# Attention steps relaid over the engines, and the softmax reciprocals turned in the value product's bank

## Chip, cores and metric

The kernel runs on one core of a Trainium2 chip. The metric is the device time of one execution in microseconds (us), as the median of several runs.

## What is computed

The reference is one transformer block on x of shape (2, 512, 256), with a modulation from c:

```
mod = (silu(c) @ wmod) -> sa, ca, ga, sb, cb, gb
h = layernorm(x) * (1 + ca) + sa
x = x + ga * attn(h)          # 32 query heads, 8 kv heads, width 64, rope, sinks, window of 128
h = layernorm(x) * (1 + cb) + sb
h2 = h + attention(rmsnorm(h))  # 32/8 heads again, causal over 512, no window
x = x + gb * (h2 + moe(rmsnorm(h2)))   # 8 experts, top 2
```

Everything is float32; the kernel splits each matmul operand into a high part and a low part (rounded value and rest) and adds three products: high by high, low by high, high by low.

## The kernel before

**Stages.** A prologue loads and prepares; then one software pipeline of 128 attention steps runs; then routing, the experts (lines 1075 and 1096) and the output. Steps 0 to 63 are the first attention (two batches of 32 steps, called windowed), steps 64 to 127 the second (causal). The four functions `step_window` and the four `step_causal` (tensor, scalar, vector; gpsimd and sync have one `step`) write out by hand what each engine does in step u. Every engine works its own list in order; semaphores join them.

**One step u** handles a tile of 128 queries t = u % 4 of a group of four heads. `scores(u, j)` (line 882) for j = 0 to 3 fills one of two banks psS; `mask_max(u, j)` on VectorE (line 1481) adds the mask and takes the maximum; `exp_head` on ScalarE (line 1167) makes the probabilities in pbuf. Score j waits until the mask of score j - 2 has freed the bank. Two steps later `turn_probs(u, k)` (line 892) transposes key tile k into a bank psX, ScalarE copies its high part (`probs_hi`, pTh), VectorE subtracts to get the low part (`probs_lo`, line 1497, pTl), and `values(u, k)` (line 917) multiplies with v and adds up in psO. A windowed tile has one or two key tiles, a causal one up to four.

**The division.** `denominator(u)` on VectorE makes rden, the four reciprocals of a row (in the windowed steps with a term of the sink: `sink_in` on GpSimd, line 682, an exp on ScalarE, and den, line 1489). GpSimd spreads rden over 256 columns (`spread`, line 694, rdenx), TensorE turns that (`turn_scale`, line 900), ScalarE copies it to rS (`scale_of`), and VectorE multiplies psO by rS (`scale_out`, line 1503, oS). ScalarE copies the high part oh (`out_hi`), GpSimd subtracts (`out_low`, line 687), and `out_project` (line 933) adds the product with wo in psY.

**Projections.** `ahead(u)` names the piece of a coming group's q, k or v that step u computes: 14 of 16 steps have one (a run of 16 steps is a quad; m = u % 16). `project_q`, `project_k` and `project_v` (lines 817, 830, 847) write the bank psP. The turned scale of `turn_scale` and the turned features of `turn_features` (line 859) are written into psP too, so a projection first waits until ScalarE has copied rS out of it (`begin_item`):

```
                if u is not None and u >= 2:
                    pe.wait_ge(a_rx, min(u - 1, NU))
```

The windowed half sends a q or k piece through `rope` on VectorE (lines 1448 and 1450), then GpSimd adds, copies the high part and subtracts (lines 661 to 675) into st. In the causal half ScalarE and VectorE split it straight from psP into st. SyncE stores st to DRAM (qd, kd) and loads it back in another layout (qE, kT), one buffer of st being used by all. The weights are loaded raw and split on GpSimd (`split_wq`, `split_wkv`, `split_wo`: a copy, then a subtraction).

## Time and profile before

| | us |
|---|---|
| median of 3 runs | 1406.89 (1406.08 to 1414.29) |
| the profiled execution, whole | 1400.63 |
| its span, first to last instruction | 1398.7 |

In the page of the profile, PE is TensorE's matmuls and PEld its weight loads, DVE VectorE, ACT ScalarE, POOL GpSimd. Over the span PE was busy 1064.0 us (76%), DVE 792.3 (57%), ACT 712.4 (51%) and POOL 478.8 (34%), and the mean granted TensorE clock was 0.905 of full speed. A matmul's end is modelled, so busy PE says that matmuls were in flight. "Idle before" is how long the engine stood still just ahead of a group of instructions; "issue" is what the profile gives where it finds no releaser.

### The profile page before, as it was taken

Reading aid. Unit: us, or ns where it says so; the run is one execution under the profiler, and the core shown is the slowest. Engines: PE = TensorE matmul, PEld = TensorE weight load, DVE = VectorE, ACT = ScalarE, POOL = GpSimd, SP = SyncE. Lnnn points to the kernel's source line nnn. Section 1 sums busy time; section 2 is a strip of 40 time slices with the busy share of each in tenths; the row PEclk is TensorE's granted clock in tenths of the full one; section 3 lists DMA queues with packets and bytes.
Section 4 is the critical chain, followed back from the end, with each engine's and each line's share of the span. In section 5 each row is a group of like instructions: output and inputs, shape, how many; then the busy total and the mean of one; then the engine's idle time right before and its main releaser. Section 6 shows DMA issues by size and latency. Waiting matters only on the chain.

```text
span 1398.7 us, 22967 instructions
## 1 busy us (share of the span) xinstructions
PE 1064.0 (76%) x6836; PEld 946.2 (68%) x6836; DVE 792.3 (57%) x2276; ACT 712.4 (51%) x2003; POOL 478.8 (34%) x659
## 2 busy tenths in 40 slices
PE   3647767777775677779878999988899726889893
PEld 1336666667665566668767888877788616888883
DVE  4445565555555554456655666656666553666655
ACT  2124535455453454566665666675676523555541
POOL 2355544755653454244222424322222140000003
PEclk7778978999997798999999999999999957999997
DMA  6455445545731343454344345534332063555513
GB/s 144 124 121 166 129 128 140 164 131 163 168 93 46 98 123 96 132 135 142 89 123 99 99 121 135 145 84 128 84 88 49 1 227 105 155 144 151 151 39 104
DMA packets 151823, 166.58 MB, mean 119 GB/s; under 512 B 79572, under 2 KB 108180, under 8 KB 146580
## 3 DMA queue, kind: packets, MB, share of 16 engines
q1 hardware_dynamic: 129427, 143.27, 38.8%
q10 hardware_dynamic: 20736, 17.64, 3.9%
q0 software_dynamic: 1536, 4.20, 0.9%
q8 instruction: 57, 0.93, 0.3%
q14 instruction: 67, 0.54, 0.1%
HBM read 106.28 MB, written 58.79 MB: 118 GB/s over the span
## 4 chain that ended last, share of the span: by engine, by line
PE 37%; issue 8%; DVE 6%; ACT 4%; DMA 3%; POOL 2%; ACTq 1%; SPq 0%; DVEq 0%; POOLq 0%
PE psO L917 7%; PE psS L882 5%; PE psX L892 4%; PE psP L817 4%; PE psS L1075 3%; PE psX L1075 3%; PE psY L933 3%; DMA kd<-st 2%; PE psO L1096 2%; PE psP L1096 2%; ACT pTh L1136 1%; DVE pbuf L1481 1%; PE psP L900 1%; DVE pTl L1497 1%; POOL xg L766 1%
## 5 line engine op out<-in xcount | busy, mean ns | idle before, releaser
L1167 ACT ACTIVATE pbuf<-pbuf,nmax 128x256 f32<-128x256 f32 (+3 forms) x512 | 265.5, 519 | 298.0 <-DVE nmax L1481 296.7
L1481 DVE CUSTOM_DVE_ANT_0 pbuf<-psS,mcau 128x256 f32<-128x256 f32 (+3 forms) x512 | 215.4, 437 | 55.8 <-PE psS L882 52.4
L1497 DVE TENSOR_TENSOR pTl<-psX,pTh 128x512 fp32r<-128x512 f32 x272 | 187.5, 689 | 76.0 <-ACT pTh L1136 73.4
L882 PE MATMUL psS<-kT,qE 128*128 128x256 f32 (+3 forms) x1024 | 214.6, 320 | 11.2 <-DVE nmax L1481 10.9
L687 POOL TENSOR_TENSOR ol<-oS,oh 128x256 fp32r<-128x256 f32 x128 | 94.7, 740 | 332.9 <-ACT oh L1136 332.7
L917 PE MATMUL psO<-pTh,vpad 128*128 128x256 f32 x1088 | 192.4, 300 | 13.5 <-DVE oS L1503 6.4
L1136 ACT ACTIVATE pTh<-psX 128x512 fp32r<-128x512 f32 x272 | 159.6, 587 | 51.0 <-PE psO L917 48.7
L882 PEld LDWEIGHTS psS<-kT,qE 128*128 128x128 f32 x1024 | 157.3, 202 | 24.4 <-DVE nmax L1481 22.1
L917 PEld LDWEIGHTS psO<-pTh,vpad 128*128 128x128 f32 x1088 | 151.9, 193 | 27.5 <-DVE pTl L1497 15.8
L892 PE MATMUL psX<-idn,pbuf 128*128 128x128 f32 x1088 | 169.8, 280 | 0.8 <-DVE pTl L1497 0.4
L892 PEld LDWEIGHTS psX<-idn,pbuf 128*128 128x128 f32 x1088 | 131.2, 144 | 6.8 <-DVE pTl L1497 1.6
L817 PE MATMUL psP<-hTh,wqh 128*128 128x512 f32 x128 | 62.9, 491 | 90.0 <-issue 85.5
L917 PE MATMUL psO<-pTl,vpad 128*128 128x256 f32 x544 | 110.2, 284 | 0.0
L682 POOL TENSOR_TENSOR esin<-sink_b,nmax 128x4 f32<-128x4 f32 x64 | 13.1, 204 | 254.8 <-DVE nmax L1481 254.7
L817 PEld LDWEIGHTS psP<-hTh,wqh 128*128 128x128 f32 x128 | 27.2, 213 | 106.4 <-issue 96.8
L1167 ACT ACTIVATION_READ_ACCUMULATOR pbuf<-pbuf,nmax 128x1 f32 x512 | 97.0, 189 | 0.0
L1136 ACT ACTIVATE oh<-oS 128x256 fp32r<-128x256 f32 x128 | 53.4, 417 | 76.5 <-DVE oS L1503 76.5
L917 PEld LDWEIGHTS psO<-pTl,vpad 128*128 128x128 f32 x544 | 85.1, 192 | 0.0
L933 PE MATMUL psY<-woh,oh 128*128 128x256 f32 x256 | 79.6, 311 | 1.1 <-POOL ol L687 1.1
L1448 DVE SCALAR_TENSOR_TENSOR tmp<-psP,bq,cosT 128x512 f32<-128x512 f32 x32 | 24.0, 751 | 96.5 <-PE psP L817 96.5
L933 PE MATMUL psY<-woh,ol 128*128 128x256 f32 x256 | 78.6, 307 | 0.0
L775 POOL DMA_INDIRECT hb<-yg,slots_out x8 | 8.4, 1045 | 204.7 <-DMA yg<-modb 202.5
(225 smaller groups left out, 2465.7 us busy)
## 6 DMA issues: line engine op xcount, KB each, us to landing
qd<-st SPq DMA_DIRECT2D x32, 1024.0 KB, 4.3
qE<-qd SPq DMA_DIRECT2D x128, 256.0 KB, 5.7
mrawV<-in_w_moe SPq DMA_DIRECT2D x32, 384.0 KB, 3.3
mrawB<-in_w_moe SPq DMA_DIRECT2D x32, 384.0 KB, 3.4
kT<-kd SPq DMA_DIRECT2D x64, 128.0 KB, 2.9
kT<-kd SPq DMA_DIRECT2D x32, 256.0 KB, 4.1
kd<-st SPq DMA_DIRECT2D x7, 1024.0 KB, 8.2
xg<-sq ACTq DMA_DIRECT2D x7, 640.0 KB, 3.4
```

What stands on the lines that cost most here:

```text
L687: G.tensor_tensor(ol[:, u % 2, :], oS[:, u % 2, :], oh[:, u % 2, :], ALU.subtract).then_inc(g_ol, 1)
L817: last = mm(psP[:, :], w[:, g % 2, k, i * P:(i + 1) * P], a[:, k, b * SEQ:(b + 1) * SEQ], start=(n == 1), stop=(n == 3 * KC))
L882: last = mm(psS[j % 2][:, 0:n], qE[:, g % 2, j, t * P:(t + 1) * P], kT[:, g % 2, c, k0:k0 + n], start=(c == 0), stop=(c == 1))
L892: last = turn(psX[kt % 2][:, j * P:(j + 1) * P], probs(u, j)[:, k * P:(k + 1) * P], idn[:, :])
L917: last = mm(psO[:, 0:2 * P], vpad[:, quad % 2, c, kv, at:at + 2 * HD], pairs(pT)[:, r], start=(k == 0 and n == 0), stop=(k == keys(u) - 1 ...
L933: last = mm(psY[t // 2][:, t % 2 * D:(t % 2 + 1) * D], a[:, u % 2, i * P:(i + 1) * P], w[:, g % 2, i * D:(i + 1) * D], start=(first and n ...
L1075: last = mm(ps[f % 2][:, 0:TP], w[:, at:at + P], a[:, k, :], start=(n == 1), stop=(n == 3 * KC))
L1096: last = mm(psD[m][:, 0:TP], w[:, at:at + P], a[:, f % NR, :], start=(f == 0 and n == 0), stop=(f == NF - 1 and n == 2))
L1136: copy = lambda o, i: nc.scalar.activation(o, i, ACT.Copy)
L1167: nc.scalar.activation(pj, pj, ACT.Exp, bias=nmax[:, u % 4, j:j + 1], scale=-1.0, accum_out=sums[:, u % 4, j:j + 1]).then_inc(a_exp, 1)
L1481: V.tensor_tensor_reduce(probs(u, j), psS[j % 2][:, 0:n], mcau[:, SEQ - n:], -SCALE, 3e38, ALU.add, ALU.min, nmax[:, u % 4, j:j + 1]).then ...
L1497: V.tensor_tensor(pTl[:, kt % 2, :], psX[kt % 2][:, :], pTh[:, kt % 2, :], ALU.subtract).then_inc(v_pl, 1)
```

## The change

1. **Bank of the reciprocals.** `turn_scale` writes the upper half of psO instead of psP, and belongs to step u - 3 instead of u - 2. `begin_item` no longer waits for rS.
2. **TensorE's order.** In a windowed step both `turn_probs` come right after the first score, the last value product of u - 3 after the second, `turn_scale` and the projection between the third and the fourth, `out_project` (now of u - 5) after it, and the first value product last. The causal step is relaid too. The loop runs one step longer.
3. **Copies go to ScalarE.** The high parts of the weights (`high_wq`, `high_wkv`, `high_wo`) and of rope's result (`rope_high`) are made by ScalarE; GpSimd keeps the sums and the subtractions. `sink_in` goes from GpSimd to VectorE. The reciprocals are made a step later and spread (u - 1 in GpSimd's order).
4. **Takes.** VectorE takes the projection of step u at the start of step u + 1. The feature turns go two tiles at a time through the slots without a projection.
5. **SyncE** has its loads and stores at new steps.

```diff
     quad, m = divmod(u, QUAD)
+    if u % SEGU in (15, 18):
+        return ("f", 2 * (u // SEGU + 1) + (u % SEGU == 18), 0)
...
-def turned(u):
-
-    seg, r = divmod(u, SEGU)
-    if r not in (14, 15):
-        return ()
-    return tuple(TB * (seg + 1) + 2 * (r - 14) + i for i in range(2))
-
...
             store_q(1)
             place_q(1)
             load_wq(3)
-
-            def step(u):
+
...
+
                 quad, m = divmod(u, QUAD)
-                g = u // TB
-                for at, part in ((3, 2), (5, 3), (12, 4), (15, 5)):
-                    if m == at and 4 * quad + part < NG:
-                        store_q(4 * quad + part)
-                if m % TB == 0 and g + 1 < NG:
-                    place_k(g + 1)
-                    if g >= 1:
+                g = 4 * quad
+                if m == 0:
+                    if quad:
+                        store_q(g + 1)
+                        place_k(g + 1)
...
+                        low_wq(4 * quad + part)
+                for at, part in ((1, 0), (5, 1), (9, 2), (13, 3)):
+                    if m == at and 4 * quad + part > 0:
+                        low_wo(4 * quad + part)
+                if m == 2 and quad + 1 < NQUAD:
+                    low_wkv(quad + 1, 1)
+                if m == 10 and quad + 2 < NQUAD:
+                    low_wkv(quad + 2, 0)
+
+            def rope_sum(pair):
                 pool.wait_ge(v_pj, ITEM[pair + (1,)])
                 apart(pool)
...
-                pool.wait_ge(g_pa, 2 * n)
-                apart(pool)
-                G.tensor_copy(st[:, 0, 0, :], tmp[:, 0, :]).then_inc(g_ph, 1)
-                G.tensor_copy(st[:, 0, 1, :], tmp[:, 2, :]).then_inc(g_ph, 1)
                 n = TURN[pair]
-                pool.wait_ge(g_ph, 2 * n)
-                apart(pool)
-                G.tensor_tensor(st[:, 1, 0, :], tmp[:, 0, :], st[:, 0, 0, :], ALU.subtract).then_inc(g_pl, 1)
-                G.tensor_tensor(st[:, 1, 1, :], tmp[:, 2, :], st[:, 0, 1, :], ALU.subtract).then_inc(g_pl, 1)
...
-            def sink_in(u):
-                pool.wait_ge(v_max, QM * (u + 1))
-                wait(pool, a_es, u - 3)
-                apart(pool)
-                g = u // TB % NKV
-                G.tensor_tensor(esin[:, u % 4, :], sink_b[:, g * QM:(g + 1) * QM], nmax[:, u % 4, :], ALU.add).then_inc(g_es, 1)
+                for r in range(2):
...
             def step(u):
-                quad, m = divmod(u, QUAD)
                 seg, r = divmod(u, SEGU)
-                if 0 <= u - 1 < 2 * SEGU:
-                    sink_in(u - 1)
                 if 0 <= u - 4 < NU:
                     out_low(u - 4)
-                if 0 <= u - 2 < NU:
-                    spread(u - 2)
+                if seg in (1, 2) and 3 <= r < 3 + TB:
+                    residual(TB * (seg - 1) + r - 3)
...
-                    if seg in (0, 2) and 20 <= r < 25:
-                        gate_rows(GA if seg == 0 else GB, r - 20)
+                    low_weights(u)
+                if turns(u):
+                    rope_sum(ahead(u)[:2])
+                if 0 <= u - 1 < NU:
+                    spread(u - 1)
+                if seg in (0, 2) and 20 <= r < 25:
...
-                    pe.wait_ge(a_rx, min(u - 1, NU))
-
-            def project_q(g, i, u=None):
-                begin_item(("q", g, i), u)
+
...
             def turn_scale(u):
                 pe.wait_ge(g_rx, u + 1)
-                pe.wait_ge(v_pj, BANKED[min(u + 1, NU - 1)])
-                wait(pe, a_rx, u)
                 for i in range(2):
-                    last = turn(psP[:, i * P:(i + 1) * P], rdenx[:, i * P:(i + 1) * P], idn[:, :])
+                    last = turn(psO[:, (2 + i) * P:(3 + i) * P], rdenx[:, i * P:(i + 1) * P], idn[:, :])
                 last.then_inc(s_rx, 1)
...
                 last.then_inc(s_Y, 1)
             def step_window(u):
-                item = ahead(u) if u < NU else None
-                old = 0 <= u - 2 < NU
-                nk = keys(u - 2) if old else 0
+                nk = keys(u - 2) if u >= 2 else 0
+                scores(u, 0)
                 if nk > 0:
                     turn_probs(u - 2, 0)
-                if 0 <= u - 3 < NU:
-                    values(u - 3, keys(u - 3) - 1)
-                scores(u, 0)
-                scores(u, 1)
-                if old:
-                    turn_scale(u - 2)
                 if nk > 1:
                     turn_probs(u - 2, 1)
-                if item:
-                    project(item, u)
-                if 0 <= u - 4 < NU:
-                    out_project(u - 4)
+                scores(u, 1)
+                if u >= 3:
+                    values(u - 3, keys(u - 3) - 1)
                 scores(u, 2)
+                if u >= 3:
+                    turn_scale(u - 3)
+                if ahead(u):
+                    project(ahead(u))
                 scores(u, 3)
+                if u >= 5:
+                    out_project(u - 5)
                 if nk > 1:
                     values(u - 2, 0)
-                for n in turned(u):
-                    turn_features(n, u)
...
                 now = u < NU
-                item = ahead(u) if now else None
                 nk = keys(u - 2) if u - 2 < NU else 0
                 if now:
                     scores(u, 0)
                 if nk > 0:
                     turn_probs(u - 2, 0)
-                    turn_scale(u - 2)
                 if now:
                     scores(u, 1)
+                if u - 3 < NU:
+                    values(u - 3, keys(u - 3) - 1)
+                if now:
+                    scores(u, 2)
+                if u - 3 < NU:
+                    turn_scale(u - 3)
                 if nk > 1:
                     turn_probs(u - 2, 1)
-                if u - 3 < NU:
-                    values(u - 3, keys(u - 3) - 1)
-                if item:
-                    project(item, u)
-                if u - 4 < NU:
-                    out_project(u - 4)
+                if now:
+                    scores(u, 3)
+                if now and ahead(u):
+                    project(ahead(u))
                 if nk > 2:
                     turn_probs(u - 2, 2)
-                if now:
-                    scores(u, 2)
                 if nk > 1:
                     values(u - 2, 0)
+                if nk > 2:
+                    values(u - 2, 1)
                 if nk > 3:
                     turn_probs(u - 2, 3)
-                if nk > 2:
-                    values(u - 2, 1)
-                if now:
-                    scores(u, 3)
+                out_project(u - 5)
                 if nk > 3:
                     values(u - 2, 2)
-                if now:
-                    for n in turned(u):
-                        turn_features(n, u)
             pe.wait_ge(v_cb, KC * BATCH)
             modulation(0)
             modulation(1)
             turn_trig()
-            for t in range(TB):
...
                 wait(act, v_os, u - 1)
-                copy(rS[:, u % 2, :], psP[:, 0:2 * P]).then_inc(a_rx, 1)
+                copy(rS[:, u % 2, :], psO[:, 2 * P:4 * P]).then_inc(a_rx, 1)
             def out_hi(u):
                 act.wait_ge(v_os, u + 1)
...
+            def high_weights(u):
+                quad, m = divmod(u, QUAD)
+                for at, part in ((0, 3), (4, 4), (8, 5), (12, 6)):
+                    if m == at and 4 * quad + part < NG:
+                        high_wq(4 * quad + part)
+                for at, part in ((1, 0), (5, 1), (9, 2), (13, 3)):
+                    if m == at and 4 * quad + part > 0:
+                        high_wo(4 * quad + part)
+                if m == 2 and quad + 1 < NQUAD:
+                    high_wkv(quad + 1, 1)
+                if m == 10 and quad + 2 < NQUAD:
+                    high_wkv(quad + 2, 0)
+
+            def rope_high(pair):
+                n = TURN[pair]
+                if PAIR[pair] > 0:
+                    act.wait_ge(st_out, OUT[PAIR[pair] - 1])
+                for r in range(2):
+                    act.wait_ge(g_pa, 2 * n - 1 + r)
+                    copy(st[:, 0, r, :], tmp[:, 2 * r, :]).then_inc(a_rh, 1)
...
                 item = ahead(u)
                 nk = keys(u - 2) if u >= 2 else 0
-                if u >= 1:
-                    sink_exp(u - 1)
+                high_weights(u)
                 if nk > 0:
                     probs_hi(u - 2, 0)
                 exp_head(u, 0)
                 if u >= 3:
-                    out_hi(u - 3)
-                if nk > 0:
-                    scale_of(u - 2)
+                    scale_of(u - 3)
                 if nk > 1:
                     probs_hi(u - 2, 1)
+                if u >= 4:
+                    out_hi(u - 4)
                 exp_head(u, 1)
                 if item and by_scalar(item):
                     high(item)
                 exp_head(u, 2)
+                if u >= 1:
+                    sink_exp(u - 1)
+                if turns(u - 1):
+                    rope_high(ahead(u - 1)[:2])
                 exp_head(u, 3)
                 between(u)
-                for n in turned(u):
...
+                if now:
+                    high_weights(u)
+                if nk > 0:
+                    probs_hi(u - 2, 0)
+                if now:
+                    exp_head(u, 0)
+                if u - 3 < NU:
+                    scale_of(u - 3)
+                if now:
+                    exp_head(u, 1)
                 if u == 2 * SEGU:
                     sink_exp(u - 1)
-                if now:
-                    exp_head(u, 0)
-                if nk > 0:
-                    probs_hi(u - 2, 0)
-                    scale_of(u - 2)
                 if nk > 1:
                     probs_hi(u - 2, 1)
                 if now:
-                    exp_head(u, 1)
-                if u - 3 < NU:
-                    out_hi(u - 3)
-                if item:
-                    high(item)
+                    exp_head(u, 2)
                 if nk > 2:
                     probs_hi(u - 2, 2)
+                if now and ahead(u):
+                    high(ahead(u))
                 if nk > 3:
                     probs_hi(u - 2, 3)
                 if now:
-                    exp_head(u, 2)
                     exp_head(u, 3)
+                if u - 4 < NU:
...
+            def sink_in(u):
+                dve.wait_ge(v_max, QM * (u + 1))
+                wait(dve, a_es, u - 3)
+                g = u // TB % NKV
+                V.tensor_tensor(esin[:, u % 4, :], sink_b[:, g * QM:(g + 1) * QM], nmax[:, u % 4, :], ALU.add).then_inc(v_es, 1)
...
-                item = ahead(u)
                 nk = keys(u - 2) if u >= 2 else 0
+                if u >= 1 and ahead(u - 1):
+                    take(ahead(u - 1))
+                mask_max(u, 0)
+                if u >= 2:
+                    denominator(u - 2)
+                mask_max(u, 1)
                 if u >= 1:
-                    denominator(u - 1)
-                mask_max(u, 0)
-                mask_max(u, 1)
+                    sink_in(u - 1)
+                mask_max(u, 2)
                 if nk > 0:
                     probs_lo(u - 2, 0)
                 if u >= 3:
                     scale_out(u - 3)
-                if item:
-                    take(item)
-                mask_max(u, 2)
                 if nk > 1:
                     probs_lo(u - 2, 1)
                 mask_max(u, 3)
                 between(u)
-                for n in turned(u):
...
             def step_causal(u):
                 now = u < NU
-                item = ahead(u) if now else None
                 nk = keys(u - 2) if u - 2 < NU else 0
+                if now and ahead(u - 1):
+                    take(ahead(u - 1))
+                if u - 3 < NU and keys(u - 3) > 3:
+                    probs_lo(u - 3, 3)
                 if now:
                     mask_max(u, 0)
-                if u - 1 < NU:
-                    denominator(u - 1)
-                if now:
                     mask_max(u, 1)
                 if nk > 0:
                     probs_lo(u - 2, 0)
+                if u == 2 * SEGU:
+                    sink_in(u - 1)
+                if now:
+                    mask_max(u, 2)
+                if u - 3 < NU:
+                    scale_out(u - 3)
+                if u - 2 < NU:
+                    denominator(u - 2)
                 if nk > 1:
                     probs_lo(u - 2, 1)
-                if u - 3 < NU:
-                    scale_out(u - 3)
-                if item:
-                    take(item)
                 if now:
-                    mask_max(u, 2)
+                    mask_max(u, 3)
                 if nk > 2:
                     probs_lo(u - 2, 2)
-                if now:
-                    mask_max(u, 3)
-                if nk > 3:
-                    probs_lo(u - 2, 3)
                 between(u)
```

## Rows read from the trace of the kernel before

**Rows 1.** Table by stretch, by 16 steps: length, busy us (count) of PE, PEld, DVE, ACT, POOL; clock, DMA share, GB/s
```profile
101.70:242.20 140.50, 104.69 (x635) 93.15 (x634) 79.05 (x242) 63.61 (x214) 68.27 (x98) 0.85 0.52 141
242.20:366.10 123.90, 95.63 (x628) 84.36 (x625) 66.74 (x229) 62.06 (x209) 75.72 (x104) 0.93 0.57 153
366.10:515.00 148.90, 103.36 (x636) 91.87 (x634) 83.64 (x263) 71.34 (x228) 75.94 (x107) 0.86 0.38 96
515.00:636.20 121.20, 93.05 (x611) 82.20 (x610) 60.21 (x217) 66.24 (x215) 47.89 (x77) 0.93 0.46 125
636.20:770.60 134.40, 110.99 (x750) 99.02 (x749) 82.03 (x246) 85.30 (x234) 41.35 (x60) 0.96 0.40 107
770.60:884.70 114.10, 105.58 (x742) 94.09 (x741) 72.26 (x214) 76.08 (x216) 42.99 (x57) 1.00 0.47 125
884.70:1012.10 127.40, 109.60 (x750) 97.43 (x749) 77.71 (x228) 82.13 (x230) 33.78 (x50) 0.97 0.39 106
1012.10:1102.40 90.30, 82.73 (x596) 72.98 (x595) 58.39 (x175) 63.83 (x179) 21.67 (x36) 1.00 0.21 54
```

**Rows 2.** Groups by line and operation: count, busy us, mean ns, idle us before and its releasers
```profile
L817 PE MATMUL psP<-hTh,wqh 128*128 128x512 f32 x128 | 62.9, 491 | 90.0 <-issue 85.5 <-DVE tmp L1450 3.3 <-DVE hTl L1459 1.0
...
L847 PE MATMUL psP<-wkvh,hTh 128*128 128x256 f32 x64 | 22.4, 350 | 49.2 <-issue 40.4 <-DVE vpad L1464 6.4 <-DVE biasv L1645 2.4
```

**Rows 3.** Timeline, start and length in us, from one projection to the next and on
```profile
571.88 0.47 PE L817 MATMUL psP<-hTh,wqh 128*128 128x512 f32 x1 [1.50 <-issue]
...
573.35 0.28 PE L933 MATMUL psY<-woh,oh 128*128 128x256 f32 x1
...
578.30 0.44 PE L900 MATMUL psP<-idn,rdenx 128*128 128x128 f32 x2 [0.29 <-POOL rdenx L694]
...
579.40 0.41 DVE L1503 TENSOR_TENSOR oS<-psO,rS 128x256 f32<-128x256 f32 x1
...
579.85 0.42 ACT L1136 ACTIVATE oh<-oS 128x256 fp32r<-128x256 f32 x1 [0.68 <-DVE oS L1503]
...
580.17 0.37 ACT L1136 ACTIVATE rS<-psP 128x256 f32<-128x256 f32 x1
...
580.64 0.77 PE L817 MATMUL psP<-hTh,wqh 128*128 128x512 f32 x1 [1.90 <-issue]
...
583.34 0.40 PE L933 MATMUL psY<-woh,oh 128*128 128x256 f32 x1
...
584.17 0.64 PE L882 MATMUL psS<-kT,qE 128*128 128x256 f32 x4
584.65 0.60 PE L892 MATMUL psX<-idn,pbuf 128*128 128x128 f32 x4
585.00 0.72 PE L917 MATMUL psO<-pTh,vpad 128*128 128x256 f32 x4
...
585.79 0.63 PE L882 MATMUL psS<-kT,qE 128*128 128x256 f32 x4
```

**Rows 4.** Groups by line again: VectorE's mask, low part and rope; GpSimd's `sink_in`
```profile
L1481 DVE CUSTOM_DVE_ANT_0 pbuf<-psS,mcau 128x256 f32<-128x256 f32 (+3 forms) x512 | 215.4, 437 | 55.8 <-PE psS L882 52.4 <-DVE vare L1427 0.3 <-issue 0.3
...
L1497 DVE TENSOR_TENSOR pTl<-psX,pTh 128x512 fp32r<-128x512 f32 x272 | 187.5, 689 | 76.0 <-ACT pTh L1136 73.4
...
L1448 DVE SCALAR_TENSOR_TENSOR tmp<-psP,bq,cosT 128x512 f32<-128x512 f32 x32 | 24.0, 751 | 96.5 <-PE psP L817 96.5
...
L682 POOL TENSOR_TENSOR esin<-sink_b,nmax 128x4 f32<-128x4 f32 x64 | 13.1, 204 | 254.8 <-DVE nmax L1481 254.7
```

**Rows 5.** Timeline of a windowed step with feature work: GpSimd and VectorE
```profile
201.38 1.44 POOL L662 TENSOR_TENSOR tmp<-tmp 128x512 f32<-128x512 f32 x1
201.62 1.22 DVE L1489 TENSOR_TENSOR den<-sums,esink 128x4 f32<-128x4 f32 x1
```

**Rows 6.** Groups by line again: a ScalarE copy of 512 columns
```profile
L1136 ACT ACTIVATE st<-psP 128x512 fp32r<-128x512 f32 x40 | 23.5, 588 | 20.2 <-PE psP L817 8.1 <-DMA kd<-st 4.3 <-DMA qd<-st 4.1
```

**Rows 7.** DMA issues: queue, count, KB of one, median us from issue to landing
```profile
qd<-st SPq DMA_DIRECT2D x32, 1024.0 KB, 4.3
```

300 lines of the change are left out of this document (174 added, 126 removed).

## The prediction

> **What bounds the kernel now.** I read the table by stretches first, then the groups by line with their idle time, then the timeline of one step, last the waits of SyncE's queue and the DMA issues. The stretches run from the copy of rS in step 2 to that in each 16th step after it; the last has 15 steps. The 64 windowed steps take 140.5 + 123.9 + 148.9 + 121.2 = 534.5 us, 8.35 each. In them PE is busy for 104.7 + 95.6 + 103.4 + 93.1 = 396.7 us, so no matmul is in flight for 137.8 us, and the granted clock is 0.85 to 0.93. No other engine is nearer to full: in the second stretch VectorE is busy 66.7 / 16 = 4.17 us of a step of 7.74, ScalarE 3.88, GpSimd 4.73. The 63 causal steps take 134.4 + 114.1 + 127.4 + 90.3 = 466.2 us with PE busy for 408.9, and the clock stands at 0.96 to 1.00 [rows 1]. So the windowed half is paced by a chain across the engines, the causal half nearly by TensorE.
>
> Which chain, the idle column tells: 85.5 us before the first matmul of a q piece and 40.4 before that of a v piece, put down to "issue" [rows 2]. The timeline shows what "issue" hides. From one q piece to the next are 8.76 us (571.88 to 580.64). `turn_scale` begins at 578.30; then nothing runs on TensorE until 580.64, 1.90 us. In between come oS on VectorE (579.40), oh (579.85) and rS (580.17) on ScalarE, and 0.1 us behind the end of rS the projection starts [rows 3]. That is the wait in `begin_item`: psP holds the turned scale, and ScalarE, in its order, copies it only behind oh of another tile, which waits for VectorE. Behind the projection wait the third and fourth score, their masks, the exps, the sink, den and rdenx, and behind those the next `turn_scale`: it is a loop, once around per step.
>
> TensorE's own work in such a step, by starts: projection 571.88 to 573.35 = 1.47; `out_project` 583.34 to 584.17 = 0.83; two scores 584.17 to 584.65 = 0.48, so 0.96 for four; a turn 0.35, two 0.70; a value product 585.00 to 585.79 = 0.79, two 1.58; `turn_scale` 0.44. Sum 5.98 us of 8.76. And the waits cost twice: the projection behind the 1.90 us takes 580.64 to 583.34 = 2.70 us, the lower of the clock's levels (1.2 GHz), against 1.47 at the upper (2.4 GHz) [rows 3].
>
> **The change, part by part.** *Bank of the reciprocals:* the wait of the projection on rS is gone. `turn_scale` of u - 3 comes after the third score; its rdenx is spread in GpSimd's step u - 2, so the 0.29 us that it waited for rdenx [rows 3] goes too. What is late next: the first value product of u - 2 may not start before oS of u - 3 has left psO. From the start of the third score that chain is 0.24 + `turn_scale` 0.44 + rS 0.37 + oS 0.41 = 1.46 us [rows 3]; by VectorE's order it is 0.24 + mask 0.44 + low part 0.69 + oS 0.41 = 1.78 [rows 3, 4]. TensorE meanwhile does 0.24 + 0.44 + 1.47 + 0.24 + 0.83 = 3.22 us. Cover 1.4 us; without a projection (2 steps of 16) it is 1.75 against 1.78, about even. I cost it at nothing.
>
> *VectorE* now must close a loop: masks of step u, `take` of its piece, first mask of u + 1, third score, projection. Its work in a q step: four masks 4 x 0.437 = 1.75, two low parts 1.38, oS 0.41, rope 2 x 0.75 = 1.50, and three instructions on 128x4 (den, reciprocal and the new `sink_in`) at the 0.204 of `sink_in` on GpSimd [rows 3, 4]. Sum 5.65, under TensorE's 5.98; other steps have less, since only 10 of 16 hold a q or k piece. A den with GpSimd at work on rope's sums took 1.22 us, and ended as that GpSimd instruction did (201.62 + 1.22 = 202.84 against 202.82) [rows 5]. So `sink_in` on VectorE costs between nothing and 1.22; I take 0.2, for most GpSimd instructions are short and the copies leave GpSimd. By the Trainium skill (SBUF — State Buffer, section "SBUF: two separate sides") VectorE and GpSimd contend for one pair of ports, held for a whole instruction, and a VectorE instruction with two SBUF inputs blocks behind a GpSimd one; by that rule, moving `sink_in` to VectorE speaks against this change. The one row agrees with it; what it would make of the sum is the first rival.
>
> *ScalarE* gains, per 16 windowed steps, 10 copies of weights and 10 of rope at 0.588 [rows 6]: 11.8 us or 0.74 a step, 3.88 + 0.74 = 4.6 [rows 1], hidden under 5.98. In the causal half it gains 0.37 on 76.08 / 16 = 4.76. If that cover were gone, 20 copies would cost 47 us in the windowed half. The copies wait for weight loads and for rope's sums, with exps queued behind them; the loads are issued about two steps (12 us) ahead. GpSimd loses those copies and `sink_in`: 4.73 falls to 3.8 or so.
>
> *SyncE:* no transfer is added. A store of st lands after 4.3 us [rows 7] and each has about three steps before st is wanted again. The DMA share would rise from 0.57 at 7.74 us a step to 0.57 x 7.74 / 5.98 = 0.74 at the new pace [rows 1]; queues lengthen, the bound is not reached. At nothing, upper end in the rivals.
>
> *Feature turns:* fewer evictions, two slots per batch of 32 steps; under 2 us in all, left at nothing. *Prologue:* five ScalarE copies stand ahead of the first exp, 0 to 5 x 0.588 = 2.9 us [rows 6]; I take 2. *Tail:* one `turn_scale` and rS after the last value product, 0.8, I take 1.
>
> **The sum.** Windowed: the new time of each stretch is what PE was busy in it, 396.7 for 534.5 us: -137.8. This sets two things against each other: as the clock rises the work shrinks below it, and some waits remain above it. It makes 6.2 us a step, a little over the 5.98 of the heaviest kind. Causal: the best stretch so far had PE busy for 105.6 / 114.1 = 92.5% with the wait still in it [rows 1]; I take 97.5%, 408.9 / 0.975 = 419.4: -46.8. Routing, experts and output stay. 1400.6 - 137.8 - 46.8 + 3 = 1219.0 on the profiled execution. The median of the runs stands at 1406.89 / 1400.63 = 1.0045 of it, so 1224.5 us. The floor, with every wait gone and the upper clock throughout: a windowed step is 5.98 less 1.14 in one of four (one key tile: a turn and a value product), less 1.47 in 2 of 16 and half of it in 4 of 16, about 5.3, so 340 us, and causal 409: 1153. My own range for this case is 1165 to 1265.
>
> **Rivals.** (a) VectorE becomes the bound. If den and `sink_in` both block for 1.0 us more in about 60% of the steps (GpSimd's busy share), a q step needs 5.65 + 1.2 = 6.9 us; 64 x 6.9 = 440, so the windowed half gives 94 and, half the causal gain lost too, the sum is 1400.6 - 94 - 23 + 3 = 1287, with the 1.0045 1292 us. For it: rows 5 and a margin of only 0.33. Against: it happens only where the two meet, and the steps without rope have room.
> (b) The stores and loads pace the steps. If a store takes 8.6 instead of 4.3 us at a DMA share of 0.74 and each of five pairs per 16 windowed steps shows the 4.3: 4 x 5 x 4.3 = 86, giving 1310 us. Against: three steps of cover.
> (c) The loop keeps its length: the masks wait for the fourth score behind the projection, `take` for the mask, the next projection for `take`; if these hops add 2.4 us to 5.98 the step is 8.35 as before, about 1405 us. By the rows they add up to VectorE's 5.65.
> (d) Slower: oS comes later than TensorE reaches the first value product by more than the 2.2 us of waits removed (0.29 + 1.90), that is over 5.4 us behind the third score, because ScalarE is held ahead of rS by an exp or a weight copy. One more us in each windowed step then gives 1400.6 + 64 = 1465 us. Against: 1.78 against 3.22.
>
> **Chances.** The forecast 0.70 (0.04 of it under 1165), (a) 0.17, (b) 0.07, (c) 0.03, (d) 0.03. The predicted time is 1224. The range that holds it 8 times in 10 reaches from 1165 through (a) and (b) to 1310. A measurement tells about 1% from no change here: faster by over 1% 0.94, within 1% 0.03, slower by over 1% 0.03.
>
> **What would show it.** Right: no "issue" idle before the projections (125.9 us now); windowed steps of about 6.2 us, clock above 0.95 there; PE over 90% busy in both halves; the first value product waiting less than 10 us in all for oS. Wrong: PE idle before the third score, released by the mask (a, c); den and `sink_in` near 1.2 us on the mean (a); ScalarE copies waiting for DMA or qE late at a group's first score (b); value products waiting for oS in most steps (d).

## The result: 1151 us for 1408.5

The changed kernel takes 1150.99 us (median of 4 runs, 1148.96 to 1156.19), beside 1408.51 (1406.08 to 1414.29) for the kernel before: a ratio of 0.817 [0.814, 0.821]. The forecast was 1224 with a range from 1165. The direction and the places were right, the gain was 257 us where 182 had been worked out, and the time lies under the range.

The table by stretch of the changed kernel answers [rows 1]. Its stretches again run from a copy of rS to the sixteenth after it; the copy for tile u is now made in step u + 3, before in u + 2. The columns are those of [rows 1]: length, busy us (count) of PE, PEld, DVE, ACT, POOL; clock, DMA share, GB/s.

```profile
107.13:194.79 87.66, 82.60 (x622) 78.30 (x621) 81.40 (x252) 70.66 (x230) 54.07 (x61) 0.98 0.83 224
194.79:278.54 83.75, 81.39 (x625) 76.96 (x624) 75.22 (x247) 69.48 (x231) 62.59 (x68) 1.00 0.83 227
278.54:377.34 98.80, 86.96 (x634) 80.14 (x633) 88.28 (x273) 78.50 (x246) 61.25 (x71) 0.98 0.57 145
377.34:465.24 87.90, 82.51 (x617) 78.26 (x617) 65.88 (x237) 69.12 (x228) 36.75 (x48) 0.96 0.67 175
465.24:569.93 104.69, 101.40 (x750) 94.12 (x749) 78.81 (x243) 87.63 (x240) 36.72 (x51) 1.00 0.54 137
569.93:668.48 98.55, 98.40 (x742) 92.98 (x741) 71.06 (x217) 79.13 (x225) 37.85 (x48) 1.00 0.58 145
668.48:769.34 100.86, 99.96 (x750) 94.00 (x749) 73.60 (x225) 83.30 (x235) 29.22 (x41) 1.00 0.50 134
769.34:852.33 82.99, 81.17 (x618) 75.06 (x617) 56.86 (x171) 62.27 (x176) 20.75 (x33) 1.00 0.24 58
```

The same view with one row for each half, first the kernel before and then the changed one. These four lengths are what the experiments below are compared with.

```profile
101.70:636.20 534.50, 396.74 (x2499) 351.58 (x2499) 289.65 (x946) 263.24 (x862) 267.82 (x383) 0.89 0.48 128
636.20:1102.40 466.20, 408.90 (x2831) 363.52 (x2830) 290.38 (x863) 307.35 (x854) 139.79 (x203) 0.98 0.38 101
```

```profile
107.13:465.24 358.11, 333.46 (x2494) 313.66 (x2493) 310.78 (x1006) 287.76 (x927) 214.65 (x245) 0.98 0.72 191
465.24:852.33 387.09, 380.92 (x2854) 356.16 (x2853) 280.33 (x853) 312.33 (x875) 124.54 (x171) 1.00 0.48 121
```

Both halves gave: windowed 534.5 to 358.1 (-176.4, 5.60 us a step), causal 466.2 to 387.1 (-79.1, 6.14 a step). The first rS comes 5.4 us later, and behind the last one are 297.3 us against 296.3, so the rest gave nothing. (That last part is the same code in every run here; its length was between 288.1 and 297.3 us from one profiled execution to another, so half a per cent of a total says nothing by itself.) The sum, -176.4 - 79.1 + 5.4 + 1.0 = -249.1, is the difference of the spans (1398.7 and 1149.6). The idle time of TensorE went from 137.8 to 24.7 us in the first half and from 57.3 to 6.2 in the second. And its busy time fell as well, by 63.3 and 28.0, although it does the same products.

Groups by line of the changed kernel, as in [rows 2] and [rows 4]; the releasers stand behind the idle time.

```profile
L838 PE MATMUL psP<-hTh,wqh 128*128 128x512 f32 x128 | 56.5, 442 | 8.5 <-issue 3.7 <-DVE tmp L1513 3.3 <-DVE hTl L1522 1.5
...
L906 PE MATMUL psS<-kT,qE 128*128 128x256 f32 (+3 forms) x1024 | 241.0, 318 | 25.1 <-DVE nmax L1544 24.6
...
L939 PE MATMUL psO<-pTh,vpad 128*128 128x256 f32 x1088 | 182.3, 290 | 10.6 <-DVE oS L1572 8.5 <-DVE pTl L1566 1.4
...
L1558 DVE TENSOR_TENSOR den<-sums,esink 128x4 f32<-128x4 f32 x64 | 29.6, 463 | 5.7 <-ACT esink L1187 5.5
L1551 DVE TENSOR_TENSOR esin<-sink_b,nmax 128x4 f32<-128x4 f32 x64 | 26.3, 411 | 0.2 <-DVE nmax L1544 0.2
```

The 85.5 us of "issue" ahead of the q pieces are 3.7, and none is left ahead of the v pieces. Value products wait 8.5 us in all for oS. The largest wait that TensorE has left in the attention steps is for the masks, ahead of scores: 17.5 us in the windowed half, most of its 24.7 us of idle time there.

### The profile page after: what moved, and what is told of

It is laid out like the page before. It is cut to its first block, busy times and chain, and to the rows that moved or that the text cites. A ratio compares the mean times of both kernels' runs of the same rounds, so it can differ in the third digit from the quotient of the medians.

```text
span 1149.6 us, 22713 instructions
## 1 busy us (share of the span) xinstructions
PE 978.6 (85%) x6836; PEld 907.6 (79%) x6836; DVE 800.1 (70%) x2330; ACT 749.4 (65%) x2111; POOL 403.7 (35%) x477
## 4 chain that ended last, share of the span: by engine, by line
PE 65%; DVE 14%; issue 7%; ACT 6%; DMA 3%; POOL 2%; SPq 2%; ACTq 1%; DVEq 0%; POOLq 0%
PE psO L939 14%; PE psS L906 9%; PE psX L916 8%; PE psP L838 6%; PE psY L955 6%; PE psS L1089 4%; PE psX L1089 4%; DVE pbuf L1544 2%; PE psO L1110 2%; PE psP L851 2%; PE psO L922 2%; PE psP L1110 2%; PE psP L868 2%; DVE pTl L1566 1%; POOL xg L789 1%
## 5 line engine op out<-in xcount | busy, mean ns | idle before, releaser
L1544 DVE CUSTOM_DVE_ANT_0 pbuf<-psS,mcau 128x256 f32<-128x256 f32 (+3 forms) x512 | 221.7, 435 | 68.0 <-PE psS L906 64.5
L906 PE MATMUL psS<-kT,qE 128*128 128x256 f32 (+3 forms) x1024 | 241.0, 318 | 25.1 <-DVE nmax L1544 24.6
L939 PE MATMUL psO<-pTh,vpad 128*128 128x256 f32 x1088 | 182.3, 290 | 10.6 <-DVE oS L1572 8.5
L916 PE MATMUL psX<-idn,pbuf 128*128 128x128 f32 x1088 | 157.9, 275 | 6.5 <-ACT pbuf L1181 5.6
L740 POOL COPY rdenx<-rden 128x256 f32<-128x256 f32 x128 | 51.0, 398 | 180.2 <-DVE rden L1561 106.5
L1150 ACT ACTIVATE hTh<-gated 128x320 fp32r<-128x320 f32 x64 | 30.1, 471 | 71.2 <-DVE gated L1845 71.2
L1150 ACT ACTIVATE rS<-psO 128x256 f32<-128x256 f32 x128 | 48.8, 381 | 42.5 <-PE psO L922 41.8
L955 PE MATMUL psY<-woh,ol 128*128 128x256 f32 x256 | 72.5, 283 | 0.0
L955 PE MATMUL psY<-wol,oh 128*128 128x256 f32 x256 | 72.3, 283 | 0.0
L838 PE MATMUL psP<-hTh,wqh 128*128 128x512 f32 x128 | 56.5, 442 | 8.5 <-issue 3.7
```

Of the source, the lines that this page charges most:

```text
L740: G.tensor_copy(rdenx[:, :].rearrange("p (h d) -> p h d", h=QM), rden[:, u % 4, :].unsqueeze(2).broadcast_to([P, QM, HD])).then_inc(g_rx, 1)
L838: last = mm(psP[:, :], w[:, g % 2, k, i * P:(i + 1) * P], a[:, k, b * SEQ:(b + 1) * SEQ], start=(n == 1), stop=(n == 3 * KC))
L906: last = mm(psS[j % 2][:, 0:n], qE[:, g % 2, j, t * P:(t + 1) * P], kT[:, g % 2, c, k0:k0 + n], start=(c == 0), stop=(c == 1))
L916: last = turn(psX[kt % 2][:, j * P:(j + 1) * P], probs(u, j)[:, k * P:(k + 1) * P], idn[:, :])
L939: last = mm(psO[:, 0:2 * P], vpad[:, quad % 2, c, kv, at:at + 2 * HD], pairs(pT)[:, r], start=(k == 0 and n == 0), stop=(k == keys(u) - 1 ...
L955: last = mm(psY[t // 2][:, t % 2 * D:(t % 2 + 1) * D], a[:, u % 2, i * P:(i + 1) * P], w[:, g % 2, i * D:(i + 1) * D], start=(first and n ...
```

## Experiments

Each run was compared with the kernel before, at 1409 to 1410 us in its own set. "Windowed" and "causal" are the lengths of the two halves, measured as above. Edits of "before" start from the kernel before, all others from the changed kernel.

### The bank and the order, each without the other

**The bank alone.** In the kernel before, `turn_scale` writes the upper half of psO and belongs to u - 3, behind the last value product. ScalarE's copy of rS moves with it, and in a windowed step it now stands ahead of oh instead of behind it. Everything else keeps its order.

```diff
                 if 0 <= u - 3 < NU:
                     values(u - 3, keys(u - 3) - 1)
+                    turn_scale(u - 3)
                 scores(u, 0)
                 scores(u, 1)
-                if old:
-                    turn_scale(u - 2)
...
-                    last = turn(psP[:, i * P:(i + 1) * P], rdenx[:, i * P:(i + 1) * P], idn[:, :])
+                    last = turn(psO[:, (2 + i) * P:(3 + i) * P], rdenx[:, i * P:(i + 1) * P], idn[:, :])
...
-                    pe.wait_ge(a_rx, min(u - 1, NU))
...
                 if u >= 3:
+                    scale_of(u - 3)
                     out_hi(u - 3)
-                if nk > 0:
-                    scale_of(u - 2)
```

> The kernel before with one part of the change: turn_scale of u - 3 writes the upper half of psO, right behind the last value product, and the projection no longer waits for rS. Orders, copies and takes stay as before. Theory 1 (the wait on rS was the chain): most of the windowed gain comes, 1407 goes to about 1200 to 1270, and the idle time ahead of the projections falls from 126 us to under 30. Theory 2 (the chain re-closes at once through the masks behind the projection, so that only the whole relaying opens it): 1350 or more, the idle time moves to the scores and to ScalarE's exps.

Measured: 1282.68 us, ratio 0.910 [0.907, 0.913]; windowed 435.4 (-99.1), causal 453.5 (-12.7). Groups by line, first two of the kernel before and then those of this run:

```profile
L882 PE MATMUL psS<-kT,qE 128*128 128x256 f32 (+3 forms) x1024 | 214.6, 320 | 11.2 <-DVE nmax L1481 10.9
L917 PE MATMUL psO<-pTh,vpad 128*128 128x256 f32 x1088 | 192.4, 300 | 13.5 <-DVE oS L1503 6.4 <-DVE pTl L1497 5.5
```

```profile
L880 PE MATMUL psS<-kT,qE 128*128 128x256 f32 (+3 forms) x1024 | 221.8, 325 | 47.2 <-DVE nmax L1475 46.3
L913 PE MATMUL psO<-pTh,vpad 128*128 128x256 f32 x1088 | 197.4, 305 | 57.2 <-DVE pTl L1491 38.0 <-DVE oS L1497 17.1
...
L815 PE MATMUL psP<-hTh,wqh 128*128 128x512 f32 x128 | 58.9, 460 | 14.1 <-issue 9.8 <-DVE tmp L1444 3.3 <-DVE hTl L1453 1.0
...
L845 PE MATMUL psP<-wkvh,hTh 128*128 128x256 f32 x64 | 21.4, 334 | 8.8 <-DVE vpad L1458 6.4 <-DVE biasv L1639 2.4
```

The 85.5 and 40.4 us of "issue" ahead of the projections [rows 2] are 9.8 and none: the reading of the wait was right. But the time is 13 us over the band of the theory that the wait is the whole loop, because a good part of it turned into other waits: 57.2 us ahead of value products (for the low part and for oS) and 47.2 ahead of scores (for a mask), where it was 13.5 and 11.2 before. In the old order they stand too close behind their producers. That part of the gain is not the bank's. How much of the 126 us comes from ScalarE's copy standing ahead of oh, and not from the bank itself, this run doesn't tell: the copy moved in the old bank was not tried.

**The order with the wait put back.** The changed kernel, with TensorE waiting for the newest rS ahead of each projection (the causal step has the same line):

```diff
                 if ahead(u):
+                    wait(pe, a_rx, u - 2)
                     project(ahead(u))
```

> The changed kernel, with one wait put back: the projection waits until ScalarE has copied rS of the scale turned just before it. Theory 1: the wait costs 0.5 to 2 us in each of the steps with a projection, so 1151 goes to 1220 to 1330. Theory 2 (in the new order ScalarE has nothing of another tile ahead of rS, so the wait is short): turn 0.14 + copy 0.38 us and the hops, 0.6 us x 112 = under 70 us, 1200 to 1220.

Measured: 1188.43 us, ratio 0.843 [0.841, 0.845]; windowed 387.5, causal 400.7. The group of the q pieces:

```profile
L838 PE MATMUL psP<-hTh,wqh 128*128 128x512 f32 x128 | 58.5, 457 | 36.3 <-ACT rS L1152 27.6 <-issue 3.7 <-DVE tmp L1515 3.3
```

Less than either theory gave: +37 us. The wait is still there, but it costs 27.6 us over 64 q pieces, 0.43 each, against 1.90 in [rows 3]; ahead of the v and k pieces stand another 7.6 and 3.8. ScalarE now copies rS right behind its first exp and not behind oh, which itself waited for VectorE. That reading fits the listing: the loop was made of the wait and of what stood in ScalarE's order between. No run tests ScalarE's order by itself. The two runs together:

| median, us | old order | new order |
|---|---|---|
| projection waits for rS | 1409 | 1188 |
| no such wait | 1283 | 1151 |

Taking the wait away gives 126 us in the old order and 37 in the new; the rest of the change, which I call relaying, gives 221 with the wait and 132 without. In the lengths of the two halves alone it is 112 and 43, 212 and 144. Relaying is the larger part. Two limits: "new order" holds the moved copies and SyncE's new steps too, and with the wait put back the reciprocals are still in psO. So `turn_scale` is still spared what it waited for in the kernel before, that VectorE had taken the last projection out of psP. The new order with the bank of before was not run; its 1188 is the case with the wait alone.

### Which part of the order

**TensorE's windowed order of before**, all other engines as changed:

```diff
-                scores(u, 0)
                 if nk > 0:
                     turn_probs(u - 2, 0)
-                if nk > 1:
-                    turn_probs(u - 2, 1)
-                scores(u, 1)
                 if u >= 3:
                     values(u - 3, keys(u - 3) - 1)
-                scores(u, 2)
-                if u >= 3:
                     turn_scale(u - 3)
+                scores(u, 0)
+                scores(u, 1)
+                if nk > 1:
+                    turn_probs(u - 2, 1)
                 if ahead(u):
                     project(ahead(u))
-                scores(u, 3)
                 if u >= 5:
                     out_project(u - 5)
+                scores(u, 2)
+                scores(u, 3)
```

> The changed kernel with TensorE's order of before in the windowed steps (first turn and last value product first, the scores in two pairs around the projection, turn_scale right behind the value product); all else as changed. Bank alone had given the windowed half 435 us, the changed kernel 358. Theory P (TensorE's order made the rest): about 420 to 435 us in the windowed half, 1151 goes to 1210 to 1230. Theory V (the take at the start of the next step, and the later sink and reciprocals, made it): within 15 us of 358, 1150 to 1165.

Measured: 1210.85 us, 0.858 [0.855, 0.861]; windowed 422.7 (+64.6), causal 387.0 (unchanged). The group of the value products:

```profile
L939 PE MATMUL psO<-pTh,vpad 128*128 128x256 f32 x1088 | 189.3, 296 | 76.1 <-DVE oS L1571 74.5 <-DVE pTl L1565 1.4
```

Here is the wait that rival (d) spoke of: value products wait 74.5 us for oS (72.2 of them in the windowed half, 1.1 us a step), and the half is 64.6 us longer. A q step of this run shows how:

```profile
250.70 0.38 PE L922 MATMUL psO<-idn,rdenx 128*128 128x128 f32 x2
...
252.47 0.36 ACT L1149 ACTIVATE rS<-psO 128x256 f32<-128x256 f32 x1
...
253.94 0.64 PE L906 MATMUL psS<-kT,qE 128*128 128x256 f32 x4
254.48 0.42 DVE L1543 CUSTOM_DVE_ANT_0 pbuf<-psS,mcau 128x256 f32<-128x256 f32 x1 [0.77 <-PE psS L906]
...
254.83 0.68 DVE L1565 TENSOR_TENSOR pTl<-psX,pTh 128x512 fp32r<-128x512 f32 x1
255.44 0.41 DVE L1571 TENSOR_TENSOR oS<-psO,rS 128x256 f32<-128x256 f32 x1
...
255.91 0.74 PE L939 MATMUL psO<-pTh,vpad 128*128 128x256 f32 x4 [1.33 <-DVE oS L1571]
```

The projection still stands between `turn_scale` and the value product, and rS is ready 2.6 us before oS starts. But VectorE makes oS behind the mask of the third score and a low part, and the third score now comes only behind the projection and `out_project`. From its start to the value product are 1.97 us (the prediction's sum by VectorE's order was 1.78), and TensorE has only two scores to put in between. So what hides the wait in the new order is that the third score comes before the projection. The bank makes this wait possible. Whether VectorE could make oS ahead of that mask instead was not tried.

**All causal orders of before** (TensorE, ScalarE and VectorE; the reciprocals stay in psO). The core of the edit on TensorE:

```diff
+                    values(u - 3, keys(u - 3) - 1)
+                    turn_scale(u - 3)
+                if item:
+                    project(item)
...
+                if now:
+                    scores(u, 2)
                 if nk > 1:
                     values(u - 2, 0)
...
+                if now:
+                    scores(u, 3)
                 if nk > 3:
                     values(u - 2, 2)
```

> The changed kernel with the causal steps in the orders of before on TensorE, ScalarE and VectorE (bank, copies and SyncE's steps as changed). The causal half took 466 us before, 453 with the bank alone, 387 changed. If the orders made the gain: 445 to 455 and 1151 goes to 1210 to 1225. If the copies, the reciprocals' place or SyncE's steps made it: under 400 and under 1165.

Measured: 1194.82 us, 0.847 [0.843, 0.851]; windowed 361.0, causal 433.2 (+46.1), between the two theories. The table of its two halves:

```profile
106.48:467.47 360.99, 334.98 (x2501) 314.40 (x2500) 311.72 (x1008) 289.42 (x930) 216.45 (x247) 0.99 0.71 189
467.47:900.68 433.21, 399.28 (x2847) 357.74 (x2846) 285.53 (x851) 310.89 (x874) 122.69 (x169) 1.00 0.42 108
```

Two things. More than half of the causal gain of 79.1 is the order of the step: 46.1. The bank gives 13 or so (12.7 in the old order, 400.7 - 387.1 = 13.6 in the new); the 20 that remain lie in what this run keeps of the change (copies, loads, feature turns, the later `out_project`). One piece shows in the idle times: with the bank alone TensorE stands still for 10.9 us in the causal half ahead of `turn_features`, here for nothing. The rest I did not take apart. And PE is "busy" for 399.3 us here and for 380.9 in the changed kernel, with the same products, the same clock of 1.00 and the same weight loads (357.7 and 356.2). Busy PE holds modelled ends: where a gap follows a matmul its whole modelled length counts, where another follows only the distance between the starts does. It is no measure of the work. The Trainium skill (Perfetto Trace Analysis, section "Identifying the Most-Contended Engine") says that matmul busy time is no good measure of how near a kernel is to the engine's limit, and that the busy share of weight loads is one, beside the share of peak arithmetic. This pair of runs agrees: 5% apart in the one, 0.4% in the other.

**The take in the same step**, windowed half only: VectorE takes the projection of u after oS in step u, instead of first in step u + 1.

```diff
-                if u >= 1 and ahead(u - 1):
-                    take(ahead(u - 1))
                 mask_max(u, 0)
...
                     scale_out(u - 3)
+                if ahead(u):
+                    take(ahead(u))
```

> The changed kernel, but in the windowed steps VectorE takes the projection of step u in step u, ahead of the last low part and the fourth mask, as the kernel before did. Theory V: the take again stands between the projection and the masks, 1.5 us in 12 of 16 steps at most, 1151 goes to 1190 to 1225. Theory P: VectorE comes to it when the projection is nearly done anyway, under 15 us, to 1165 at most.

Measured: 1160.38 us, 0.822 [0.819, 0.826]; windowed 370.3 (+12.2), causal 387.3. Under 15 us, as theory P had it. The loop of rival (c), from mask to take to projection, doesn't show even here: no q, k or v piece of the windowed half waits for a take, with it or without. What grows is the wait of scores for masks (17.5 to 20.4 us in that half), the wait of turns for a low part (none to 2.7), and TensorE's busy time (333.5 to 339.7). The take delays what stands behind it on VectorE.

### The moves between engines

**High copies back on GpSimd** (weights and rope, as before; the core of it for rope):

```diff
+                for r in range(2):
+                    G.tensor_copy(st[:, 0, r, :], tmp[:, 2 * r, :]).then_inc(a_rh, 1)
...
-                if turns(u - 1):
-                    rope_high(ahead(u - 1)[:2])
```

> The changed kernel, with the copies of the high parts (weights and rope) back on GpSimd. If their move carried part of the gain (VectorE blocked less, weights ready earlier): 1170 to 1200. If it is hidden work on either engine: within 1% of 1151.

**`sink_in` back on GpSimd:**

```diff
-                if u >= 1:
-                    sink_in(u - 1)
...
+                if 0 <= u - 1 < 2 * SEGU:
+                    sink_in(u - 1)
```

> The changed kernel, with sink_in back on GpSimd. VectorE loses 64 x 0.41 = 26 us of work. If VectorE is a bound of the windowed half: 5 to 20 us faster. If TensorE is: within 0.5% of 1151, or some us slower, as the sink's exp on ScalarE now waits for GpSimd's queue.

**Both back:**

> The changed kernel with both the copies of the high parts and sink_in back on GpSimd. Each alone was 7 and 5 us faster than 1151. If they add: 1139. If GpSimd is then late with weights, rope or sinks: 1150 or more.

Measured: copies back 1143.59 us, 0.811 [0.809, 0.814], windowed 360.2 and causal 385.9; `sink_in` back 1146.19, 0.813 [0.812, 0.815], windowed 352.4 and causal 387.1; both back 1145.53, 0.811 [0.808, 0.814], 358.1 and 385.9. None costs anything, and they don't add: each alone kept to its second theory (within 1%, within 0.5%), and both together lie between the two. To see whether a half per cent is real, the changed kernel and the one with the copies back were run once more side by side, in five rounds:

> The changed kernel as it is, beside the other three on one chip: 1148 to 1156.

> The changed kernel with the copies of the high parts back on GpSimd, a second time. If the 7 us of the first time are real: 1141 to 1146, its interval clear of the changed kernel's. If they were the chip's spread: within 3 us of the changed kernel.

Measured: 1151.11 us, 0.817 [0.814, 0.819], against 1145.25, 0.813 [0.810, 0.816]. The intervals overlap, and the two halves are 357.8 + 387.1 against 359.3 + 386.0, so no gain lies in the steps; behind the last rS they differ by 7.5 us, 297.3 against 289.8, in code that is the same. Whether these variants beat the changed kernel by some 0.5% stays open; the moves between the engines are not where the 257 us come from. That agrees with the forecast, which costed them near nothing.

VectorE's small instructions are longer beside GpSimd, as [rows 5] suggested. `sink_in` takes a mean of 411 ns on VectorE and 202 on GpSimd. Lengths of one tile's instructions, first of the changed kernel and then with `sink_in` back (ns: min/median/max):

```profile
L1551 DVE TENSOR_TENSOR esin<-sink_b,nmax x64: 152/292/795, 90.0 to 450.1; 128x4 f32<-128x4 f32 x64
...
L1558 DVE TENSOR_TENSOR den<-sums,esink x64: 150/162/1201, 100.9 to 456.4; 128x4 f32<-128x4 f32 x64
L1561 DVE RECIPROCAL rden<-den x64: 177/178/180, 101.1 to 456.5; 128x4 f32<-128x4 f32 x64
```

```profile
L735 POOL TENSOR_TENSOR esin<-sink_b,nmax x64: 191/202/226, 99.4 to 446.8; 128x4 f32<-128x4 f32 x64
```

Set beside GpSimd's instructions in the same trace, the spread sorts itself. The 28 den instructions that start with nothing in flight on GpSimd take 0.15 to 0.16 us, without exception. The 36 that start beside one have a mean of 0.70, and 20 of them end within 0.06 us of that GpSimd instruction's end. The reciprocal, which reads one tile instead of two, never leaves 177 to 180 ns. By the Trainium skill (SBUF — State Buffer, section "SBUF: two separate sides") an instruction of VectorE with two SBUF inputs is blocked behind one of GpSimd that reads SBUF; these lengths agree with it. The price of having `sink_in` on VectorE is small: its removal gave 5.7 us of the windowed half by itself, and 1.3 to 2.2 with the copies on GpSimd too (358.1 against 360.2 and 359.3).

### Is a resource the bound?

**Less work for TensorE.** `out_project` leaves out its third product (oh by the low part of wo), 2 of its 6 matmuls, 0.24 us a step by the starts:

```diff
-                    for a, w in ((oh, woh), (ol, woh), (oh, wol)):
+                    for a, w in ((oh, woh), (ol, woh)):
```

> The changed kernel without the third product of out_project (high part of the output by low part of wo): 2 of 6 matmuls, 0.24 us of TensorE in each of 128 steps; nothing else changes. If TensorE sets the pace of all steps: 31 us less, about 1120. If VectorE or a chain across the engines sets the windowed half: about 15 us less, from the causal half alone.

Measured: 1134.05 us, 0.804 [0.800, 0.808]; windowed 351.7 (-6.4), causal 377.8 (-9.3). The work left out is 0.24 x 64 = 15 us in each half. So in the windowed half less than half of it reaches the time, in the causal half some 60%. The total is 17 us less, near the 15 of the second theory, but it comes from both halves. In the fullest causal stretch most of it does:

```profile
563.79:659.23 95.44, 95.29 (x710) 89.49 (x709) 70.14 (x217) 78.86 (x225) 37.80 (x48) 1.00 0.60 150
```

That is 95.44 us for 98.55 with PE as full as before: 3.1 of the 3.8 us left out. TensorE is the bound there. In the windowed half the waits for oS grow instead (6.4 to 10.5 us), so chains through VectorE and ScalarE share in setting the pace. VectorE alone doesn't set it either: `sink_in` back on GpSimd took 17 us of work off it and the half got 5.7 shorter. The third windowed stretch of the changed kernel says the same: VectorE is busy for 88.28 of its 98.80 us, TensorE for 86.96.

**More work for the DMA engines.** In each second of the first 32 steps one more DMA writes 640 KB from SBUF to a spare buffer in DRAM:

```diff
+                if seg == 0 and r % 2 == 0:
+                    act.dma_start(spare[r // 2], sq[:, :].unsqueeze(1).broadcast_to([P, 5, D])).then_inc(st_more, 16)
```

> The changed kernel with 16 more DMAs of 640 KB in the first 32 steps (zeros to a spare DRAM buffer), 10 MB beside some 38 MB there: the DMA share of the first two stretches would go from 0.83 to about 1.0. If the stores and loads already pace these steps: 15 to 35 us more, in those two stretches. If TensorE does and the transfers are covered: under 8 us more.

Measured: 1150.42 us, 0.816 [0.812, 0.819]. The two stretches that hold 14 of the 16 additional transfers:

```profile
108.69:196.20 87.51, 81.71 (x622) 76.92 (x621) 81.45 (x252) 70.93 (x231) 54.86 (x62) 1.00 0.95 281
196.20:279.94 83.74, 81.42 (x625) 76.99 (x625) 75.22 (x247) 69.80 (x231) 62.59 (x68) 1.00 0.95 279
```

The share goes from 0.83 to 0.95 and the stretches stay (87.66 and 83.75 without the additional transfers). Transfers do take longer to land there (by the median xg from 4.5 to 7.2 us and kT from 4.5 to 5.2; the stores of q stay, 5.3 and 5.2), but the steps are no longer for it. DMA is not the bound in these two stretches, and the share is lower in all others.

## The prediction, point by point

**What bounds the kernel, and "issue" read as the wait on rS: right, but not whole.** The bank alone takes the idle time ahead of q pieces from 85.5 to 9.8 us of "issue". But the loop closed through other waits as well, as its 57.2 and 47.2 us show; the step-by-step account took 1.90 and 0.29 us as the only waits to remove. The second was right in size: 22.7 us of idle time ahead of `turn_scale` for rdenx in the windowed half, 0.35 a step, and none in the changed kernel. A third, ahead of `turn_features`, was left out (see "The rest"). More than half of what the causal half gained is order, and I had put all of it down to the wait.

**The first value product covered: right.** 1.78 against 3.22 us was the sum; the wait is 8.5 us in all (I had given under 10), and with the projection moved ahead of the third score it is 74.5. The sum rightly counted from the third score: VectorE's order sets the chain.

**VectorE's work in a q step, and rival (a): the size of `sink_in` was off, the conclusion was right.** I took 0.2 us, measured 0.41; den had a mean of 0.46. The two together cost 0.47 a step more than taken, VectorE is busy for 310.8 of 358.1 us, and of rival (a)'s 1.2 us of price per q step 0.47 is there as work, while taking `sink_in` off VectorE gives 0.09 a step.

**Rival (c):** its sign shows in part. TensorE's idle time ahead of scores, for masks, is 17.5 us in the windowed half, where it was 2.4 before. That is 0.27 a step for the 2.4 that (c) needed.

**Rival (b): once.** The one wait of the kind in the step of 10.4 us (the mean is 5.6), in the timeline of ScalarE:

```profile
400.87 0.60 ACT L1150 ACTIVATE st<-psP 128x512 fp32r<-128x512 f32 x1 [6.24 <-DMA qd<-st]
```

The copy of a k piece waits for st, which a store of the pair before still holds. The 6.2 us are all the idle time that stores give this group of copies, and no score waits for a load. The stores' median time to landing is 4.5 us, for 4.3 in [rows 7].

**The pace of the windowed half: the step that failed.** I set the new time equal to what PE had been busy, 396.7 us, and it is 358.1, 38.6 less. That busy time was itself made by the waits. It holds matmuls at the lower clock level (mean granted clock 0.89, now 0.98) and modelled ends ahead of gaps. As an estimate, 396.7 x 0.89 / 0.98 = 360.3, so the clock makes some 36 of the 63.3 us by which it fell, and the closed gaps the other 27. The sum of 5.98 us for a q step, which made 6.2 a step look like a fair pace, holds terms that were read in stretches with waits. The timeline of TensorE in the changed kernel, from one `turn_scale` of a q step to the next, has none of them:

```profile
262.81 0.41 PE L922 MATMUL psO<-idn,rdenx 128*128 128x128 f32 x2
262.97 0.48 PE L838 MATMUL psP<-hTh,wqh 128*128 128x512 f32 x1
...
264.46 0.33 PE L906 MATMUL psS<-kT,qE 128*128 128x128 f32 x2
264.63 0.33 PE L955 MATMUL psY<-woh,oh 128*128 128x256 f32 x1
...
265.39 0.64 PE L939 MATMUL psO<-pTh,vpad 128*128 128x256 f32 x4
...
266.11 0.40 PE L906 MATMUL psS<-kT,qE 128*128 128x256 f32 x2
266.35 1.03 PE L916 MATMUL psX<-idn,pbuf 128*128 128x128 f32 x8
267.14 0.48 PE L906 MATMUL psS<-kT,qE 128*128 128x256 f32 x2
267.46 0.64 PE L939 MATMUL psO<-pTh,vpad 128*128 128x256 f32 x4
...
268.18 0.40 PE L906 MATMUL psS<-kT,qE 128*128 128x256 f32 x2
268.42 0.38 PE L922 MATMUL psO<-idn,rdenx 128*128 128x128 f32 x2
```

From start to start: `turn_scale` 0.16, projection 1.49, a score 0.17, `out_project` 0.76, value product 0.72, score 0.24, two turns 0.79, score 0.32, value product 0.72, score 0.24. Sum 5.61. Against the 5.98: `turn_scale` -0.28, two value products -0.14, `out_project` -0.07 (its start was read at a granted clock of 0.84), turns +0.09, the rest +0.03. The largest miss is `turn_scale`, where I had taken the modelled length of 0.44, which stood ahead of a gap, and not the distance to a next start. A step of 5.61 with the prediction's own deductions (two turns less one and a value product, 1.12, in one of four; 1.49 in 2 of 16 and half of it in 4 of 16) is 5.61 - 0.28 - 0.37 = 4.96, or 317 us for 64. The measured 358.1 lies 41 over that; the forecast lay 80 over it. Of these 80, 24 are mis-sized terms (the prediction's own 5.3 a step made 341), and 56 are the choice of the old busy time over that sum. So the idle time that I expected beside the work was there (24.7 us), but the fall of the busy time, 63 us, was far larger. I had named the two as set against each other without weighing them.

**The causal half: the second step that failed, for the same reason.** The share came out as forecast or better (98.4% for 97.5%), but the 408.9 us it was applied to fell to 380.9. With the unchanged share, 380.9 / 0.975 = 390.7, within 4 us of the measured 387.1. The run with the old causal orders splits the 28.0: to 399.3 at a clock of 1.00 for 0.98 (408.9 x 0.98 = 400.7, so the clock explains it), and from there to 380.9 at the same clock with the order that has fewer gaps. The "floor" of 409 that I gave for this half, and with it the lower end at 1165, was no floor: the 1153 made from it was for the profiled execution (1158 as a median), which took 1151.5. The chance of 0.04 for a time below 1165 was too small, since it rested on a number that moves with the waits.

**The rest.** Granted clock 0.96 to 1.00 in the windowed stretches (over 0.95 forecast), PE busy 333.5 / 358.1 = 93% and 98% (over 90%), GpSimd down to 3.9 us a step in the second stretch, from which 3.8 was worked out, and ScalarE at 4.3 there (4.6): right. The feature turns, left at nothing, were not nothing: in the kernel before TensorE stood idle for 16.4 us ahead of them in the two halves (for hTl), and for nothing in the changed one. DMA share 0.83 in the first two stretches where I had 0.74, because the steps are shorter. Prologue and tail +6.4 us for +3. Against the forecast of 1219.0 for the profiled execution, which took 1151.5, the windowed half makes 38.6 of the miss, the causal half 32.3, and prologue and tail took 3.4 back.

## What to carry to other kernels

Read what an engine's work costs from the distances between starts, in a stretch where nothing waits and the granted clock is at the upper level; the busy time of a stretch with waits was above the work behind it in both halves here, and a "floor" made from it is none. A wait that sits in a loop across engines is best taken apart two ways, by removing the wait and by moving what stands between its producer and its consumer: here everything but the wait gave 221 of 1409 us, the bank alone 126, and both together 258, so what the one is worth depends on the other. Where a freed wait is replaced by a new one, follow the new chain through the order of every engine in it to where it really starts (here the third score, not `turn_scale`), and put the longest independent piece of work (here the projection) behind that start. With it ahead of that start the windowed half took 64.6 us more.

## What was unexpected of the hardware

- Busy time of TensorE for the same products at the same granted clock of 1.00 was 399.3 or 380.9 us, by the order of the work alone (weight loads 357.7 and 356.2). From start to start a value product took 0.72 us here, behind a score, and 0.79 in the kernel before, behind a turn [rows 3], both at a granted clock of 1.00.
- A DMA share of 0.95, at 280 GB/s, left the steps and the landing of the q stores (5.2 us, before 5.3) where they were at 0.83 and 225 GB/s. Other transfers landed up to 2.7 us later, and the schedule had room for it.
- den, an instruction of VectorE on 128x4 with two SBUF inputs, takes 0.16 us with GpSimd idle at its start and up to 1.20 with GpSimd at work; the reciprocal behind it, with one input, always 0.18. The move of `sink_in` changed the half of 64 steps by at most 5.7 us in all, far less than the spread of single instructions suggests.
